# A cross-attention and mixture-of-experts kernel on one core: the first tiles of two experts run between attention and experts, on the rows known by then

## What is computed

```python
def reference(x, ctx_1024, g_xattn, g_ffn, ...):
    ...
    x = x + jnp.tanh(g_xattn[0]) * _L0_xattn_ref(_layernorm(x), ctx_1024, ctx_1024, ...)   # 16 heads of 16
    x = x + jnp.tanh(g_ffn[0]) * _L0_ffn_ref(_layernorm(x), ...)
    return x

    def _L0_ffn_ref(hidden_states, conf_w, conf_b, gate_w, up_w, down_w, wealth):
        E, K = (8, 2)
        confidences = jax.nn.sigmoid(jnp.einsum('bsh,eh->bse', x, conf_w) + conf_b)
        bids = confidences * wealth
        top_bids, selected_experts = jax.lax.top_k(bids, K)
        ...
        routing_weights = jax.nn.softmax(top_bids, axis=-1)
        combine = jnp.sum(jax.nn.one_hot(selected_experts, E) * routing_weights[..., None], axis=2)
        def ffn(gw, uw, dw):
            return down(jax.nn.silu(gate(x)) * up(x))        # 256 -> 1024 -> 256
        output = jnp.einsum('ebsh,bse->bsh', jax.vmap(ffn)(gate_w, up_w, down_w), combine)
```

## Time and profile before

| | |
|---|---|
| median of three runs | 1199.79 us (1197.14 to 1202.4) |
| profiled execution | 1202.42 us, its span 1200.6 us |
| TensorE, VectorE, ScalarE, Pool busy in the span | 1091.6, 668.0, 555.3, 315.6 us |
| mean granted clock of TensorE | 0.961 of 2.4 GHz |
| products of further tiles (L1287, L1299, L1301) | 2048 + 1024, 512, 512 matmuls: 32 further tiles |
| adds to the output | 8 of first tiles, 64 of further ones, two each |

### The profile page before, as it was taken

The page is one execution under the profiler, slowest core; times in us unless marked ns, Lnnn a source line. Parts: engine busy times, 40 slices in busy tenths (PEclk is TensorE's granted clock), DMA queues, the critical chain, the costliest instruction groups (busy, mean ns, idle before and its releaser), DMA issues. The chain is left out here.

```text
span 1200.6 us, 24032 instructions
## 1 busy us (share of the span) xinstructions
PE 1091.6 (91%) x8213; PEld 896.2 (75%) x8213; DVE 668.0 (56%) x1588; ACT 555.3 (46%) x891; POOL 315.6 (26%) x366
## 2 busy tenths in 40 slices
PE   5789999999999988289899999999989999999994
PEld 4456666666666655247599999999849999999994
DVE  2546777777777774365644444444564444444442
ACT  3456676666676664155533333333453333333331
POOL 2122444444343332311311122112221122112111
PEclk8899999999999997589999999999999999999998
DMA  8100111111111101384621121112141122112111
GB/s 297 52 15 24 39 37 44 48 46 37 37 37 37 44 30 48 121 317 164 220 56 32 22 36 32 28 30 36 31 140 28 22 36 36 31 23 36 32 26 23
DMA packets 48025, 72.85 MB, mean 61 GB/s; under 512 B 6256, under 2 KB 42864, under 8 KB 44912
## 3 DMA queue, kind: packets, MB, share of 16 engines
q0 software_dynamic: 16896, 43.53, 14.2%
q1 hardware_dynamic: 30000, 27.68, 7.8%
q10 hardware_dynamic: 1088, 1.11, 0.3%
HBM read 47.14 MB, written 24.90 MB: 60 GB/s over the span
## 5 line engine op out<-in xcount | busy, mean ns | idle before, releaser
L1519 POOL DMA_INDIRECT out<-y,token x64 | 104.6, 1634 | 473.1 <-DVE y L1453 364.1
L1379 ACT ACTIVATE silu<-gate 128x512 f32<-128x512 f32 x128 | 76.5, 597 | 277.4 <-PE up L1287 277.4
L1299 PE MATMUL down<-w_split,h_hi 128*128 128x512 f32 x512 | 185.9, 398 | 0.0
L901 DVE TENSOR_REDUCE max_neg<-maxps 128x4 f32<-128x1024 f32 x128 | 156.4, 1222 | 52.8 <-PE maxps L510 51.1
L1287 PE MATMUL gate<-x_hi,w_split 128*128 128x256 f32 x1024 | 184.5, 282 | 0.0
L1287 PE MATMUL up<-x_hi,w_split 128*128 128x256 f32 x1024 | 183.8, 281 | 0.0
L1444 DVE TENSOR_TENSOR h<-silu,up 128x512 f32<-128x512 f32 x128 | 88.0, 688 | 171.4 <-ACT silu L1379 171.4
L703 ACT ACTIVATE probs<-scores 128x1024 f32<-128x1024 f32 x124 | 127.8, 1030 | 60.5 <-PE scores L535 60.5
L1287 PEld LDWEIGHTS gate<-x_hi,w_split 128*128 128x128 f32 x1024 | 148.8, 188 | 3.0
L1287 PEld LDWEIGHTS up<-x_hi,w_split 128*128 128x128 f32 x1024 | 147.8, 188 | 0.0
L1301 PE MATMUL down<-w_split,h_lo 128*128 128x256 f32 x512 | 144.2, 282 | 0.0
(11 more groups left out here) (164 smaller groups left out, 1756.3 us busy)
## 6 DMA issues: line engine op xcount, KB each, us to landing
xg<-dispatched SPq DMA_DIRECT2D x41, 272.0 KB, 2.8
stage<-gate_T POOLq DMA_DIRECT2D x8, 1024.0 KB, 7.5
stage<-up_T POOLq DMA_DIRECT2D x8, 1024.0 KB, 9.4
stage<-down_T POOLq DMA_DIRECT2D x8, 1024.0 KB, 12.0
x_all<-x SPq DMA_DIRECT2D x16, 256.0 KB, 6.3
ctxT<-ctxT SPq DMA_DIRECT2D x16, 256.0 KB, 2.7
out<-x_all SPq DMA_DIRECT2D x16, 256.0 KB, 2.1
out<-y,token POOLq DMA_INDIRECT x72, 3.8
```

The lines of the kernel that those rows point to most:

```text
L901: V.tensor_reduce(to, maxps[:], AX.X, ALU.max, negate=True).then_inc(s["max_taken"], 1)
L1299: mm(down[t][:].rearrange("p (n d) -> p n d", n=2), h_hi[:, i, rows], split[:, :, cols], start=i == 0, stop=False, skip_group_check=True)
L1379: nc.scalar.activation(silu[pair % 2][:], gate[pair % 2][:], ACT.Silu).then_inc(s_silu, 1)
L1519: pool.indirect_dma_start(out, bass.IndirectOffsetOnAxis(token[:, t:t + 1], axis=0), y[:, t, :], None, compute_op=ALU.add).then_inc(s_adde ...
```

## The change

Experts 0 and 1 get an early first tile. Padding rows are stored at places 0 to 127 of their regions at the start of the kernel (SP), and Pool waits for this before its first batch of the loop. When the last batch opens, a matmul counts the rows of batches 0 to 12 (`known_counts`), and VectorE raises both experts' running counts to at least 128 (`space_early_experts`), so that rows of batches 13 to 15 come to lie behind the first tile. SP loads both tiles of 128 rows once the scatters of batches 0 to 12 have landed. The computation of both tiles is woven into the epilogue on TensorE, ScalarE and VectorE, in gate, up and turned banks that lie over the attention's scores. Expert 1's weights are loaded in three parts after the iterations of batches 0, 1 and 14 into a second stage that is kept beside the attention's buffers; expert 2's are loaded between the last two scatters. The padding behind experts 4 to 7 is stored by Pool after its last scatter, that behind experts 0 to 3 by SP. Pool adds expert 0's early result, loads expert 3's weights, waits for that add, loads expert 4's and adds expert 1's. The expert loop then goes 2, 3, ..., 7, 0, 1, with no first tile for experts 0 and 1; if either has further tiles, its weights are rounded and split in front of them (`before_rest`), from the stage in which they are loaded once more. Buffers in both stages are listed in another order, small ones last, so that the large ones begin at multiples of 64 bytes.

```diff
+EARLY = 2
+KNOWN = 13
...
-        stage = sb(keep, "stage", [P, WCOLS])
+        stage = [sb(keep, f"stage{i}", [P, WCOLS]) for i in range(EARLY)]
...
+        early_weight = sb(keep, "early_weight", [P, 16])
+        early_token = sb(keep, "early_token", [P, 16], i32)
...
-        ITER15 = Use(without(AHEAD, NEXT), after_all(ITER14))
+        ITER15 = Use(["KNOWN"] + without(AHEAD, NEXT), after_all(ITER14))
...
+            for e in range(EARLY):
+                sp.dma_start(disp[e * REGION:e * REGION + FIRST], pads[:]).then_inc(s["first_rows_padded"], 16)
...
-            store_residual(BATCHES - 1, EPILOGUE)
-            pad_experts(sp, range(0, EXPERTS, 2))
-            sp.wait_ge(s["x2_stored"], 16 * BATCHES)
-            sp.wait_ge(s["pads_stored"], 16)
+            sp.wait_ge(s["scattered"], KNOWN * 16 * 2 * QT)
+            return (lambda: store_residual(BATCHES - 1, EPILOGUE), lambda: pad_experts(sp, range(EXPERTS // 2)))
...
+            def known_counts(use):
+                pe.wait_ge(s["rows_ready"], KNOWN)
+                use.free(pe, "KNOWN")
+                mm(use.bank("KNOWN")[:, 0, 0:EXPERTS], ones[:], macc[:], start=True, stop=True).then_inc(s["misc_written"], 1)
...
+            def space_early_experts(use):
+                use.written(dve, "KNOWN")
+                known = use.bank("KNOWN")[0:1, 0, 0:EARLY]
+                V.tensor_scalar(extra[:], known, -1.0, float(FIRST), ALU.mult, ALU.add).then_inc(s["extra_known"], 1)
+                dve.wait_ge(s["extra_known"], 1)
+                V.scalar_tensor_tensor(macc[0:1, 0:EARLY], extra[:], 0.0, macc[0:1, 0:EARLY].bitcast(fp32),
+                                       ALU.max, ALU.add).then_inc(use.freed("KNOWN"), 1)
+                use.read(dve, "KNOWN")
...
+            pool.wait_ge(s["first_rows_padded"], 16 * EARLY)
...
+                if isinstance(b, int) and b in (0, 1, BATCHES - 2):
+                    load_third(pool, 1, min(b, 2), stage[1])
+            def scatter_next_to_last():
+                scatter(BATCHES - 2, BATCHES % 2)
+            def scatter_last():
+                scatter(BATCHES - 1, (BATCHES - 1) % 2)
+                pad_experts(pool, range(EXPERTS // 2, EXPERTS))
...
+        ORDER = [*range(EARLY, EXPERTS), *range(EARLY)]
...
+            for e in range(EARLY):
+                sp.dma_start(xg[:, e], disp[e * REGION:e * REGION + FIRST]).then_inc(s_rows, 16)
+            store_last()
+            pad_low()
+            sp.wait_ge(s["pads_stored"], 16)
             attention_over(sp)
+            sp.wait_ge(s_padded[0], 16 * (EXPERTS // 2))
...
+            def early_product(e, half, mat):
+                if mat == 0 and half == 0:
+                    pe.wait_ge(s_xhi, EARLY)
+                    for n in range(2):
+                        wait_stage(pe, e, n)
+                for c in range(HC):
+                    last = mm(early_bank((gate, up)[mat], e, half)[:].rearrange("p a b -> p (a b)"),
+                              x_early[:, c, e * FIRST:(e + 1) * FIRST],
+                              weights(stages[e], mat)[:, c, half * (INNER // 2):(half + 1) * (INNER // 2)],
+                              start=c == 0, stop=c == HC - 1)
+                if mat == 1:
+                    last.then_inc(s_pair, 2)
+            def early_flip(e, half):
+                pe.wait_ge(s_made, e * PAIRS + (2 * half + 4))
+                if half == 1:
+                    pe.wait_ge(s_flipped, 2 * e + 1)
+                for i in range(IC // 2):
+                    last = nc.tensor.transpose(early_bank(gate, e, 0)[:].rearrange("p a b -> p (a b)")[:, i * P:(i + 1) * P],
+                                               h[half][:].rearrange("p a b -> p (a b)")[:, i * P:(i + 1) * P], idn[:])
+                last.then_inc(s_flip, 1)
+            def early_contract(e, half, pieces):
+                wait_stage(pe, e, 2)
+                pe.wait_ge(s_flipped, 2 * e + half + 1)
+                w = weights(stages[e], 2)
+                for i in pieces:
+                    at = half * (IC // 2) + i
+                    last = mm(early_bank(up, e, 0)[:].rearrange("p a b -> p (a b)")[:, 0:D], hT[half][:, i, :], w[:, at, :],
+                              start=at == 0, stop=at == IC - 1)
+                return last
+            turn_last_heads()
+            pe.wait_ge(s["unit_read"], handed["units"])
+            turn_rows(16 * EARLY, EARLY)
+            turn_last_normed()
+            early_product(0, 0, 0)
+            project_last_out()
+            early_product(0, 0, 1)
+            early_product(0, 1, 0)
+            early_product(0, 1, 1)
+            turn_last_x2()
+            early_flip(0, 0)
+            last_logits()
+            early_contract(0, 0, (0, 1))
+            early_flip(0, 1)
+            early_contract(0, 0, (2, 3))
+            early_contract(0, 1, range(IC // 2)).then_inc(s_down, 1)
+            last_ranks()
+            early_product(1, 0, 0)
+            count_rows()
+            early_product(1, 0, 1)
+            pe.wait_ge(s_y, TT)
+            early_product(1, 1, 0)
+            early_product(1, 1, 1)
+            early_flip(1, 0)
+            early_contract(1, 0, (0, 1))
+            early_flip(1, 1)
+            early_contract(1, 0, (2, 3))
+            early_contract(1, 1, range(IC // 2)).then_inc(s_down, 1)
+            pe.wait_ge(s_y, EARLY * TT)
+            pe.wait_ge(s_flipped, 2 * EARLY)
+            turn_rows(16 * EARLY + 16)
             over_tiles_hinted(pe, "pe_count", first, rest, before_rest)
...
+            def before_rest(e, r):
+                if e < EARLY:
+                    act.wait_ge(s_down, r + EXPERTS)
+                    for m in range(3):
+                        act.wait_ge(s_split[m], 2 * splits_before(EXPERTS))
+                    for m, half in HALVES:
+                        round_part(e + EXPERTS, m, half, s_own_hi[e])
...
+            act.wait_ge(s_turned, EARLY)
+            nc.scalar.activation(x_early[:], turned[:], ACT.Copy).then_inc(s_xhi, EARLY)
+            out_of_last()
+            early_silu(0, 0)
+            norm_last()
+            early_silu(0, 1)
+            read_last_x2()
+            read_early_flip(0, 0)
+            last_sigmoid()
+            read_early_flip(0, 1)
+            last_second_weight()
+            early_silu(1, 0)
+            early_silu(1, 1)
+            read_early_flip(1, 0)
+            read_early_flip(1, 1)
+            high_of_rows(EARLY + 1)
+            over_tiles(act, "act_count", first, rest, before_rest)
...
+            out_of_last()
+            V.memset(note[:], 0.0).then_inc(s_made, 2)
+            dve.wait_ge(s_rows, 16 * EARLY)
+            dve.wait_ge(s_xhi, EARLY)
+            V.tensor_copy(early_token[:, 0:EARLY], xg[:, 0:EARLY, TOKCOL].bitcast(i32))
+            for e in range(EARLY):
+                last = V.tensor_copy(early_weight[:, e:e + 1], xg[:, e, COMB + e:COMB + e + 1])
+            last.then_inc(s_noted, EARLY)
+            early_h(0, 0)
+            early_h(0, 1)
+            route_last()
+            dve.wait_ge(s_noted, EARLY)
+            early_y(0)
+            count()
+            early_h(1, 0)
+            early_h(1, 1)
+            early_y(1)
             attention_over(dve)
-            V.memset(note[:], 0.0).then_inc(s_made, 2)
-            rest_of_rows(1)
-            over_tiles(dve, "dve_count", first, rest)
-        def gpsimd_experts(pool):
+            rest_of_rows(EARLY + 1)
+            over_tiles(dve, "dve_count", first, rest, before_rest)
...
+            scatter_next_to_last()
+            pool.wait_ge(s["x2_stored"], 16 * BATCHES)
+            load_weights(EARLY)
+            scatter_last()
+            def add_early(e, done):
+                pool.wait_ge(s_y, e * TT + TT)
+                pool.indirect_dma_start(out, bass.IndirectOffsetOnAxis(early_token[:, e:e + 1], axis=0),
+                                        y[:, e, :], None, compute_op=ALU.add).then_inc(done, 16)
+            pool.wait_ge(s["pads_stored"], 16)
+            add_early(0, s_added)
+            pool.wait_ge(s_down, 1)
+            load_weights(EARLY + 1)
+            pool.wait_ge(s_added, 16)
+            pool.wait_ge(s_down, 2)
+            load_weights(EARLY + 2)
+            add_early(1, s_first_added)
```

More of the change, by code:

```diff
@@ L186, in attention_stage @@
         v = [sb(f"values{i}", [P, QT, HEADS, SLOT]) for i in range(2)]
-        probs = [sb(f"probs{i}", [P, HPG, QT, SEQ]) for i in range(2)]
         oS = sb("oS", [P, GROUPS, SEQ])
@@ L285, in unit, with is_last @@
             return units_before(b) + order.index(what)
+        def is_last(b):
+            return isinstance(b, int) and b == BATCHES - 1
         def has_two_homes(b):
-            return isinstance(b, int) and b == BATCHES - 1
+            return is_last(b)
         def home(b, pair):
@@ L1128, in body, with expert_stage @@
                     add_bias(b + 2)
+                if isinstance(b, int) and b in (0, 1, BATCHES - 2):
```

(45 more changed lines are left out.)

274 lines of the change are left out of this document (145 added, 129 removed).

## The result

The changed kernel took 1194.61 us (median of 8 runs, 1191.09 to 1195.87); the kernel before, run beside it, 1198.88 us (1196.91 to 1202.4). The ratio is 0.9946, 95% interval 0.9929 to 0.9963: faster by 0.5%, some 6 us, where 19.3 were forecast; the two medians are 4.3 us apart, a little less than the ratio says. 1194.6 lies above the range of 1172 to 1191. The profiled execution took 1194.51 us with a span of 1192.8, the one before 1202.42 with 1200.6. What follows accounts for the 7.8 us between these two spans.

The account below looks back on a forecast made before the run. TensorE, busy 91% of 1200.6 us, was taken as the bound, idling between last attention batch and experts. Terms -27.7 + 4.5 + 1.5 + 1.4 + 0.3 + 0.7 = -19.3 us gave 1180.5 against 1199.79; range 1172 to 1191.

Parts of the forecast that it names:

- Two first tiles move into the seam: Experts 0 and 1's first tiles fit between last attention batch and experts: -27.7 us, price of stretching 0.
- the rival of the half clock: TensorE's clock stays at half between attention and experts: +10 us, so 1190; chance 0.18.
- Three table loads: ScalarE switches Exp, Silu, Exp, Silu in the epilogue, 1.28 us per load: price 0, bounds 0 and +2.6.
- Pads at the start: Pool waits for SP's two pad tiles before its next batch, delaying everything behind: +1.4 us, bounds 0 and +3.5.
- Last third of expert 1's weights: Issued next to the shift rows, for which TensorE already waited 0.66 us: +0.7 us, bounds 0 and +2.
- the small terms: Starting pads +1.4, counting known rows +0.3, expert 1's weights +0.7: together 2.4 us ahead of expert 2's first product.
- Expert 2's weights ahead of the last scatter against half the pads: On Pool's queue, the weights' tail offset by fewer pad stores before the xg load: 0, bounds -1 and +3.
- xg landing well behind 514: Sign that the forecast is wrong: expert 2's gathered rows arriving well after 514 us.
- near 517: Sign that the forecast is right: expert 2's first product near 517 us, no first tiles of experts 0 and 1 behind it.
- The add holds, +4.5 and +1.5 of slow restart: Expert 1's add, behind 6 MB of weights, delays expert 2's further tile +4.5 us; TensorE then restarts slowly, +1.5.
- Addresses: Buffers' new places, judged by attention's projection matmuls: no effect, 0, bounds -3 and +3 us.
- the work only moves: Rival: last batch's chain queues behind expert work, giving back most of 20 us: about 1197; chance 0.08.

Follow-up runs that it names:

- run 4: Changed kernel, first tiles' padding stored behind batch 0's context load and waited for after batch 1, last third of expert 1's weights loaded after batch 1: 1194.34 us.
- run 6: run 5 plus the padding order of run 4, last third of expert 1's weights after batch 15, no second weight load for experts 0 and 1: 1178.85 us.
- run 1: Kernel before, with only the buffers of both stages listed in the changed kernel's order: 1205.2 us, ratio 1.0039.
- run 3: Changed kernel, SyncE storing only expert 2's padding before loading xg, and that of experts 0, 1 and 3 behind the load: 1191.6 us, ratio 0.9924.
- run 2: Changed kernel, Pool waiting for expert 2's gathered rows before issuing the weights of experts 3 and 4: 1191.11 us, ratio 0.9915.
- run 5: Changed kernel, only expert 2's padding ahead of its rows, both early adds first, weights of experts 3 and 4 after both its row loads landed: 1183.62 us.
- run 7: Changed kernel with 128 unused bytes ahead of w_split and 128 behind it, `note` moved into early_weight: 1188.8 us, ratio 0.9911.
- run 15: Kernel before, with 64 unused bytes behind w_split, ahead of xg, and nothing else changed: 1192.33 us, ratio 0.9918.

## Why the prediction was wrong, by its steps

*Two first tiles move into the seam, -27.7, stretch 0*: right. Both tiles were done 11.4 us behind the last rows (about 512.2), where the text had 10.8, at a granted clock of 1.00 from 475 to 514; the rival of the half clock did not come.

*Three table loads, 0*: right. Each took 1.28 us and the activation followed 1.29 or 1.30 us after its start (503.28 and 504.57), as in the earlier trace rows. The load at 493.44 on the chain began 0.02 us behind the end of the activation before it (492.82 plus 0.60). The drain that the Trainium skill, page "ScalarE: Activation LUTs", section "What ACT_TABLE_LOAD costs", adds does not show in these rows either.

*Pads at the start, +1.4*: about right; the second score unit came at 53.95 instead of 52.94, and runs 4 and 6 had the first Exp back at its old time.

*Last third of expert 1's weights, +0.7, bounds to +2*: mis-sized. SyncE's issues of the two loads of shift rows, in the changed kernel and then in the kernel before:

```profile
457.26 1.32 SPq L415 DMA_DIRECT2D queries<-max_rows  x2
```

```profile
454.75 1.32 SPq L412 DMA_DIRECT2D queries<-max_rows  x2
```

From there to the scores that wait for them it is 4.85 us (462.11) instead of 2.63 (457.38), so +2.2. In runs 1, 4 and 6, with no weights beside these loads, it is 2.64, 2.65 and 2.64. The wait itself grew by 3.2 us, 3.90 instead of 0.66, but 1 us of that is not the weights' doing: runs 1, 4 and 6 waited 1.83, 1.70 and 1.70. I took the transfer as one more in the row; 1 MB in front of it is another size. The last rows came 2.3 us later, and the small terms had been put at 2.4: that is luck, since the terms measured are larger (1.0 to 1.9 and 2.2) and traces of the same instructions have the last rows up to 2.8 us apart.

*Known counts, +0.3*: no row measures it apart.

*Expert 2's weights ahead of the last scatter against half the pads, 0, bounds -1 and +3*: at its upper bound. SyncE issued xg 3.1 us late, and the pads ended that wait. Run 3, with one pad in front, issued it 9.9 us behind the last rows instead of 13.7.

*The step that failed is the one that I did not price.* The text took the 2.8 us of xg's landing over from the earlier trace rows into the new order, while it wrote of 6 MB on Pool's queue only as something that delays an add. In the kernel before xg was issued at 509.11, 0.45 us ahead of Pool's first weights (509.56); here 3 us behind them. This cost 7.4 us. The text's own sign of being wrong, "xg landing well behind 514", came: it landed at about 524.8. Run 2 shows the cause, as it changed nothing but when the weights are issued, and xg landed in 2.7 us; run 5, which moves them too, puts expert 2's first product at 516.72, where the forecast had "near 517". The Trainium skill, page "DMA: Bandwidth & Descriptors", section "Queues, rings and completion order", says that an engine takes turns between queues packet by packet; another queue alone did not keep a load short here, at 10.2 and 16.7 us instead of about 3.

The trace of the kernel before had the price. Two of its loads of xg were issued behind weights, one at about 514.9 (DMA issues, 514 to 530 us) behind 6 MB and one at 588.44 (582 to 590 us) behind 3 MB from 582.75:

```profile
xg<-dispatched SPq DMA_DIRECT2D x1, 272.0 KB, 10.1
```

```profile
xg<-dispatched SPq DMA_DIRECT2D x1, 272.0 KB, 8.6
```

There a first tile of some 12 us stood in front of them, and TensorE did not wait for them. The other loads of xg up to 590 us, all issued ahead of weights or away from them, took 2.7 to 3.3 us. The question that the text put to the add, how it fares behind weights, was the one to put to the rows.

*The add holds, +4.5 and +1.5 of slow restart*: the +4.5 did not come, as the tile started 11 us later than the sum had it and met the add landed; the token copy at 540.22 waited for nothing. (The text's own times, 531 less 526.9, give 4.1 and not 4.5.) The add itself was as late as the text had it (near 530). Its landing, issued at 518.28:

```profile
out<-y,early_token POOLq DMA_INDIRECT x1, 14.0
```

That is 532.3. In run 2, where the tile came earlier, the add did hold the token copy, by 2.9 us. The slow start of 1.5 us came, but behind the wait for xg.

*Addresses, 0, bounds -3 and +3*: wrong, and outside its bounds. The sign was the other one: 5.8 us slower over 32 tiles. Run 1 shows 4.5 of it (0.14 us a tile) from the order of buffers alone, and run 7 took back all of it. I looked at alignment to 64 bytes in attention instead of at the distance between the operands in the experts' loop, which has 32 tiles of it. In attention the new order only made the two kinds of projection change places (run 1, as in the earlier trace rows: 396 ns from xT and 402 from the context, in place of 403 and 392), which is 0.4 us in all. With the old distance back (run 7) the kernel took 1188.8 us, inside the range of 1172 to 1191: it took this error and that of the rows' load together to leave it.

*Experts 0 and 1 at the end, 0, up to +1*: right, 0.7 us between the last add and the end.

On the sum: -19.3 as forecast, + 3.1 + 7.4 for the rows' load, - 4.5 for the hold, + 4.4 for the tiles and the rest, makes -8.9; the last add moved by -8.5. Of the rivals none was it; "the work only moves" had the size (1197), by another mechanism than the one it named.

## What to carry to other kernels

A wait that is filled with other work shows what was in its shadow: price each small transfer in the new order, by what is issued ahead of it on any queue, and put megabytes behind the last small load that someone waits for. Here it paid to issue the weights only when the loads and adds of the next tile had landed. And when buffers change places, compare the period of the innermost loop in both traces: if it moved with no instruction changed, try a few gaps between the operands' buffers.

## What was not expected of the hardware

- Products with operands declared f32r took 276 to 283 ns (128x256) when only unused bytes between their buffers changed, and a further tile 16.90 to 17.59 us: 4%, on a TensorE that is busy all the time. In run 15 the same distance of 64 modulo 256 gave 17.13 us, so the distance alone does not tell it.
- A load of 272 KB on SyncE's queue took 2.8 us when it was issued 0.45 us ahead of 6 MB of weights on Pool's queue, 2.7 with none near it (run 2), 10.2 with 3 MB ahead of it and 3 MB beside it, 16.7 among 6 MB (run 3).
- 1 MB issued 0.7 us ahead of two small loads (8 KB each) made them take 2.2 us longer, 4.85 us from issue to the work that waited for them instead of 2.63.
